# Experts' layer: four sets of tile buffers instead of two, two output buffers, weighted mask sums in other instructions, another order table

## The reference, cut to what matters

```python
q = jnp.einsum('btd,ed->bte', hidden_states, W_q)
sim = jnp.einsum('pbthn,hkpn->pbthk', q, keys)
scores_xy, idx_xy = jax.lax.top_k(sim, K)                  # K = 8 of 64 keys, twice, 4 heads
all_scores = (sx[..., :, None] + sy[..., None, :]).reshape(b, t, h, K * K)
scores, pk = jax.lax.top_k(all_scores, K)                  # 8 of the 64 pairs
de = down_embed[indices]; ue = up_embed[indices]
w = jax.nn.silu(jnp.einsum('btd,bthkd->bthk', hidden_states, de) * jax.nn.softmax(scores, axis=-1))
experts_states = jnp.einsum('bthk,bthkd->btd', w, ue)
dense = W_down @ silu(W_up @ x)                            # 512 hidden features
return dense + experts_states
```

## Time and profile before

| | |
|---|---|
| median of 3 runs | 4920.42 us (4919.32 to 4925.4) |
| the profiled execution | 4937.9 us, its span 4936.6 us |
| busy in the span | PE 86%, DVE 79%, POOL 76%, ACT 66% |
| experts' layer, first n0 to last xr | 448.4 to 1080.7 us |
| one turn of its loop in the steady state | 37.57 us |
| busy in such a turn | DVE 31.18, POOL 32.24, ACT 29.90, PE 20.61 us |
| granted clock of PE in such a turn | 0.82 |

### The profile page before, as it was taken

How to read it: one execution, slowest core, us unless ns; L and a number is a source line. 1 busy time by engine, 2 the same in 40 slices (tenths; PEclk the granted TensorE clock), 3 DMA queues, 4 the chain that set the end, 5 groups by cost and what they waited for, 6 DMA issues and landing times.

```text
span 4936.6 us, 139044 instructions
## 1 busy us (share of the span) xinstructions
PE 4239.2 (86%) x57664; PEld 3049.1 (62%) x57664; DVE 3889.2 (79%) x6375; ACT 3236.5 (66%) x5035; POOL 3775.2 (76%) x2624
## 2 busy tenths in 40 slices
PE   7886555658867899999999999999999999999997
PEld 5664444446644666666666666666666666666665
DVE  4665888855547788888888888888888888888894
ACT  4664778754434577666766767767776676767775
POOL 1113888853448899889988998889898998988993
PEclk9997778779988899999999999999999999999999
DMA  2000000000001222222222222222222222222222
GB/s 60 2 2 1 1 1 1 1 25 2 2 1 28 51 51 50 64 54 57 50 59 58 56 50 51 58 59 55 51 60 57 54 54 48 63 55 55 52 59 51
DMA packets 120832, 198.72 MB, mean 40 GB/s; under 512 B 66896, under 2 KB 78224, under 8 KB 120080
## 3 DMA queue, kind: packets, MB, share of 16 engines
q1 hardware_dynamic: 120208, 189.82, 15.7%
HBM read 24.12 MB, written 2.10 MB: 5 GB/s over the span
## 4 chain that ended last, share of the span: by engine, by line
PE 56%; ACT 14%; DVE 10%; issue 7%; POOL 6%; DMA 5%; SPq 1%; ACTq 0%; DVEq 0%; POOLq 0%
PE ps L1305 8%; PE ps L1249 8%; PE ps L1250 7%; DMA arena<-arena 5%; PE ps L1258 5%; DVE arena L1488 3%; PE ps L1346 3%; PE ps L1357 3%; PE ps L1296 2%; PE ps L1340 2%; PE ps L1297 2%; ACT L1392 2%; PE ps L1277 2%; DVE arena L1481 2%; DVE arena L598 2%
## 5 line engine op out<-in xcount | busy, mean ns | idle before, releaser
L1581 POOL TENSOR_TENSOR arena<-arena 128x1024 f32<-128x1024 f32 x384 | 909.1, 2368 | 247.7 <-DVE arena L1481 247.3
L1576 POOL TENSOR_TENSOR arena<-arena 128x32 f32<-128x32 f32 x192 | 1045.5, 5445 | 0.1
L1480 DVE TENSOR_TENSOR arena<-ps,arena 128x1024 f32<-128x1024 f32 x384 | 470.3, 1225 | 325.5 <-ACT arena L1375 325.4
L1375 ACT ACTIVATE arena<-ps 128x1024 f32<-128x1024 f32 x384 | 393.0, 1024 | 377.6 <-PE ps L1250 373.3
L1599 POOL TENSOR_TENSOR arena<-arena 128x1536 f32<-128x1536 f32 x192 | 529.1, 2756 | 114.9 <-DVE arena L1514 114.9
L208 POOL TENSOR_SCALAR arena<-arena 128x2 f32<-128x2 f32 x256 | 86.8, 339 | 630.4 <-DVE arena L202 620.4
L1305 PE MATMUL ps<-arena 96*64 96x64 f32 x12288 | 429.5, 229 | 76.1 <-DMA arena<-arena 71.6
L1305 PEld LDWEIGHTS ps<-arena 96*64 96x64 f32 x12288 | 402.8, 142 | 107.9 <-issue 99.7
L1481 DVE TENSOR_TENSOR arena<-ps,arena 128x1024 f32<-128x1024 f32 x384 | 466.5, 1215 | 0.0
L1488 DVE TENSOR_REDUCE arena<-arena 128x32 f32<-128x2048 f32 x192 | 437.0, 2276 | 0.0
L1249 PE MATMUL ps<-arena 128*128 128x512 f32 x768 | 434.3, 648 | 0.9 <-ACT arena L1424 0.9
(11 more groups left out here) (252 smaller groups left out, 9947.3 us busy)
## 6 DMA issues: line engine op xcount, KB each, us to landing
arena<-arena SPq DMA_DIRECT2D x192, 384.0 KB, 4.4
arena<-arena SPq DMA_DIRECT2D x192, 256.0 KB, 3.7
arena<-arena SPq DMA_DIRECT2D x192, 128.0 KB, 2.3
arena<-in_dWqkv SPq DMA_DIRECT2D x18, 512.0 KB, 3.6
arena<-arena SPq DMA_DIRECT2D x96, 64.0 KB
arena<-arena SPq DMA_DIRECT2D x96, 63.5 KB
arena<-in_dWo SPq DMA_DIRECT2D x6, 512.0 KB, 5.2
arena<-in_x SPq DMA_DIRECT2D x4, 512.0 KB, 7.4
```

The source lines that it names most:

```text
L1480: dve.tensor_tensor(o1, p.rearrange("p (h e) -> p h e", h=16), bc(cs, 1, 16), ALU.mult)
L1576: pool.tensor_tensor(ss[:, 0:32], ss[:, 32:64], mhalf32, ALU.pow).then_inc(*S.rs.up())
L1581: pool.tensor_tensor(a1[:, half], a1[:, half], T2[:, half], ALU.add).then_inc(*radd[g].up())
```

## The change

Five things are changed.

1. `tiles` has four sets instead of two: A and B of even batches, A and B of odd ones (`tiles[2 * (b % 2) + t]`). All waits for the reader of an earlier batch go back one batch further.
2. The normalised output lies in two buffers `out` in place of three `U.y`; n1 waits for the xr of two batches before.
3. Each of the three sums of tr is two instructions on DVE, a multiplication by a number in place and a plain addition, with a wait between them: six instructions and five waits in place of three and two.
4. PLACE has other numbers for all pieces, so another order on each engine.
5. `load_c` begins 120 words higher.

```diff
-    batches = [Batch(stats(C), sb([128, 2]), sb([128, 2, 128]), sb([128, 256]), sb([128, 4, 256]), sb([128, 2, 128]))
+    batches = [Batch(stats(C), sb([128, 2]), sb([128, 2, 128]), sb([128, 256]), sb([128, 4, 256]))
                for _ in range(NU)]
+    out = [sb([128, 2, 128]) for _ in range(2)]
...
-                  sb([128, 4, 128])) for _ in range(2)]
+                  sb([128, 4, 128])) for _ in range(4)]
...
-    PLACE = {"n0": 0, "st0": 45, "r0": 54, "hT": 120, "spcA": 193, "piA": 301, "C1A": 370, "mxA": 384, "ixA": 430,
+    PLACE = {"st0": 0, "n0": 38, "hT": 189, "spcA": 304, "spcB": 377, "r0": 416, "piA": 417, "mxA": 511, "h": 521,
...
         def tile(piece, b, t):
-            T = tiles[t]
+            T = tiles[2 * (b % 2) + t]
             ex = views(T)[3]
             if piece in ("spcA", "spcB"):
-                if b >= 1:
-                    act.wait_ge(*gp[t].at(b))
-                    act.wait_ge(*pb[t].at(b))
+                if b >= 2:
+                    act.wait_ge(*gp[t].at(b - 1))
+                    act.wait_ge(*pb[t].at(b - 1))
...
-                dve.scalar_tensor_tensor(e[:, 0:1024], e[:, 0:1024], 16.0, e[:, 1024:2048], ALU.mult,
-                                         ALU.add).then_inc(*S.step_dve.up())
-                dve.wait_ge(*S.step_dve.now())
-                dve.scalar_tensor_tensor(e[:, 0:512], e[:, 0:512], 4.0, e[:, 512:1024], ALU.mult,
-                                         ALU.add).then_inc(*S.step_dve.up())
-                dve.wait_ge(*S.step_dve.now())
-                dve.scalar_tensor_tensor(T.R, e[:, 0:256], 2.0, e[:, 256:512], ALU.mult, ALU.add).then_inc(*tr[t].up())
+                for n, w in ((1024, 16.0), (512, 4.0), (256, 2.0)):
+                    dve.tensor_scalar(e[:, 0:n], e[:, 0:n], w, None, ALU.mult).then_inc(*S.step_dve.up())
+                    dve.wait_ge(*S.step_dve.now())
+                    dve.tensor_tensor(T.R if n == 256 else e[:, 0:n], e[:, 0:n], e[:, n:2 * n], ALU.add
+                                      ).then_inc(*(tr[t] if n == 256 else S.step_dve).up())
+                    if n > 256:
+                        dve.wait_ge(*S.step_dve.now())
...
-    C.top = C.TOTAL - LAST - 1024
+    C.top = C.TOTAL - LAST - 904
```

More of the change, by code:

```diff
@@ new lines, in phase_b @@
+    PLACE = {"st0": 0, "n0": 38, "hT": 189, "spcA": 304, "spcB": 377, "r0": 416, "piA": 417, "mxA": 511, "h": 521,
+             "ixA": 523, "c8A": 576, "mxB": 582, "spA": 595, "mrA": 597, "C1A": 599, "ixB": 632, "C1B": 646,
+             "MA": 705, "nnA": 716, "c8B": 741, "ohA": 796, "mrB": 827, "eqA": 842, "piB": 863, "upc": 865,
+             "trA": 894, "spB": 898, "pcA": 909, "onA": 913, "paA": 922, "paB": 933, "xpA": 940, "txA": 953,
+             "thA": 1012, "xpB": 1014, "eqB": 1178, "pcB": 1227, "mkA": 1229, "up": 1234, "zzB": 1240, "geA": 1249,
+             "nnB": 1295, "trB": 1298, "zzA": 1331, "txB": 1393, "ohB": 1400, "MB": 1407, "sg0A": 1411, "sMA": 1425,
+             "onB": 1438, "pbA": 1461, "gpA": 1472, "sg1A": 1520, "thB": 1521, "mkB": 1596, "pbB": 1603, "geB": 1603,
+             "sg2A": 1646, "sg3A": 1647, "sg0B": 1679, "gpB": 1724, "sg1B": 2016, "atcA": 2103, "sg2B": 2213,
+             "sMB": 2295, "lsA": 2337, "sg3B": 2341, "atcB": 2470, "atA": 2494, "lsB": 2559, "st1": 2823, "n1": 2867,
+             "atB": 3155, "r1": 3250, "xr": 3453, "ot": 3459}
@@ L911, in batch @@
             if piece == "n1":
-                if b >= NU:
-                    act.wait_ge(*S.xr.at(b - NU + 1))
+                if b >= 2:
+                    act.wait_ge(*S.xr.at(b - 1))
                 act.wait_ge(*S.r1.at(b + 1))
                 p, rs = ps("ot", b), U.st[2]
-                act.activation(U.y[:, 0, :], p[:, 0:128], ACT.Identity, bias=U.nb[:, 0:1], scale=rs[:, 0:1])
-                act.activation(U.y[:, 1, :], p[:, 128:256], ACT.Identity, bias=U.nb[:, 1:2], scale=rs[:, 1:2]
+                act.activation(out[b % 2][:, 0, :], p[:, 0:128], ACT.Identity, bias=U.nb[:, 0:1], scale=rs[:, 0:1])
+                act.activation(out[b % 2][:, 1, :], p[:, 128:256], ACT.Identity, bias=U.nb[:, 1:2], scale=rs[:, 1:2]
                                ).then_inc(*S.n1.up())
         def tile(piece, b, t):
-            T = tiles[t]
+            T = tiles[2 * (b % 2) + t]
             ex = views(T)[3]
             if piece in ("spcA", "spcB"):
-                if b >= 1:
-                    act.wait_ge(*gp[t].at(b))
-                    act.wait_ge(*pb[t].at(b))
+                if b >= 2:
+                    act.wait_ge(*gp[t].at(b - 1))
+                    act.wait_ge(*pb[t].at(b - 1))
                 act.wait_ge(*sp_ps[t].at(b + 1))
@@ L989, in tile @@
         def tile(piece, b, t):
-            T = tiles[t]
+            T = tiles[2 * (b % 2) + t]
             SIM, PRJ, ey, ex, e8, eC = views(T)
             if piece in ("mxA", "mxB"):
-                if b >= 1:
-                    dve.wait_ge(*pa[t].at(b))
-                    dve.wait_ge(*C1[t].at(b))
-                    dve.wait_ge(*ix[t].at(b))
+                if b >= 2:
+                    dve.wait_ge(*pa[t].at(b - 1))
+                    dve.wait_ge(*C1[t].at(b - 1))
+                    dve.wait_ge(*ix[t].at(b - 1))
                 dve.wait_ge(*spc[t].at(b + 1))
@@ L1094, in batch @@
                 pool.wait_ge(*S.n1.at(b + 1))
-                pool.tensor_tensor(X, X, U.y, ALU.add).then_inc(*S.xr.up())
+                pool.tensor_tensor(X, X, out[b % 2], ALU.add).then_inc(*S.xr.up())
         def tile(piece, b, t):
-            T = tiles[t]
+            T = tiles[2 * (b % 2) + t]
             SIM, _, ey, ex, e8, eC = views(T)
```

78 lines of the change are left out of this document (39 added, 39 removed).

## The result

| | before | after |
|---|---|---|
| median | 4919.87 us (4918.42 to 4925.4) | 4885.85 us (4875.73 to 4890.98) |
| ratio, 95% interval | | 0.9926 [0.9908, 0.9944] |
| the same comparison again (second set of runs, on another chip) | 4931.61 us | 4887.76 us, 0.9913 [0.9900, 0.9927] |
| profiled execution, its span | 4937.9, 4936.6 us | 4875.7, 4874.4 us |
| experts' layer, first n0 to last start of xr | 448.4 to 1080.0 us | 447.4 to 1033.3 us |

The change made the kernel 34 us faster in the first comparison and 44 us in the second. The forecast was 24.6 us and a turn of 36.2. Single runs of the kernel after lie up to 15 us apart, so the layer's own time, next, measures the change better than the whole time does.

What follows compares the result with a forecast made beforehand. A loop of waits, no full engine, bounds the kernel. 14 turns from 37.57 to 36.2 (19.2 us), 1.4 at n0's third start and 4 in the drain give 24.6 us off: 4896 us, 8 in 10 within 4868 to 4927.

Steps and rivals of the forecast that it cites:

- The price of the sums: DVE's tr: six instructions taken at 2.4 us, from a range of 1.9 to 3.7, against 2.31 undisturbed for the fused three.
- a change of 0 to 0.1 us a tile: DVE's tr: what splitting the sums would change per tile, against the undisturbed 2.31 us.
- the walk: One turn of the new order followed piece by piece from the end of txA: 27.0 + r1 + 3.6, taken as 36.2 us.
- as 5.6 behind 27.0: POOL's r1 in the new turn: ends 5.6 us after st1's end at 27.0, as in the kernel before.
- spA runs 3.6: PE's spA in the new turn: takes 3.6 us behind h and hT, its copy starting 0.3 later, at 9.9.
- runs 5.45: PE's ot in the new turn: takes 5.45 us, starting 0.25 behind atcB, and ends at 26.0.
- The warning sign named for it: POOL ahead of r1: the forecast would be wrong above all if onA starts after st1.
- the rival with the queue in the products: POOL ahead of r1: late nnA puts onA, paA, paB, pcB into gpB, eqA, trA; turn 38.9, 4935 us, chance 0.14.
- R0 leaves the loop: POOL's r0: no longer closes the loop, as about 2.4 us of slack cover it before n0.
- DVE's turn: Steady turn: with r1 in 3.9 us or less DVE sets it, 34.5 us; 4870 us in all, chance 0.18.
- The drain: End of the experts' layer: DVE has 18.2 us of work in place of 22.9; 4 us counted as gain.
- If PE's clock falls under the 0.82: PE in the steady turn: a sign that the forecast is wrong, since ot and spA lie in the loop.

Runs made afterwards that it cites:

- e1: The kernel before with only four sets of tile buffers, two output buffers and load_c 120 words higher, old order and fused sums: ratio 0.9996, turn 37.38 us.
- e2: The kernel before with only the sums of tr split into six instructions: ratio 0.9954, turn 35.83 us.
- e3: The kernel after with the three fused sums put back: ratio 0.9944 to the kernel before, turn 34.80 us.
- f8: The kernel after, unchanged, run again on another chip: ratio 0.9913 to the kernel before, turn 34.09 us.
- E4: The kernel before with extra unread matmuls keeping PE busy, eight ahead of h and three behind atB: ratio 0.9957, turn 36.04 us.
- f6: The kernel after with four sets of small buffers for moments instead of three: ratio 0.9915 to the kernel before, turn 34.21 us.
- f5: The kernel after with r1 placed ahead of paA, paB and pcB on POOL: ratio 0.9927 to the kernel before, turn 34.90 us.
- g2: The kernel after with r0 alone moved ahead of oh and M on POOL: ratio 0.9942 to the kernel before, turn 36.05 us.

## Why the prediction was right, and where it was not

**Sign and range** were right: faster, within 4868 to 4927. The size was too small: 24.6 us of gain against 34 and 44 measured, and against 45.7 in the layer itself, where no other code disturbs the comparison. That 4886 lies within 10 us of the forecast 4896 is in part luck. The sum also counts 14 steady turns where its own reading of n0's starts has thirteen; with thirteen it gives 23.2 us.

**The buffers** "by themselves bring about 1 us": e1 agrees, as far as a time of 0.9996 [0.9986, 1.0006] can tell.

**The price of the sums** was right, their worth was not. The six instructions undisturbed take 0.42, 0.29 and 0.23 us for the multiplications and 0.69, 0.42 and 0.29 for the additions: 2.34 us against the 2.4 forecast. The prediction's estimate from the Trainium skill ("VectorE: DVE Perf Modes", "The perf-mode tier table") was 0.95 us for the three multiplications, and 0.94 were measured. The step that failed is "a change of 0 to 0.1 us a tile": it counted DVE's time alone. That more seams help POOL stood behind it as a remark without a number, and it was the term: e2 puts it at 1.8 us a turn in the old order, e3 at 0.7 in the new one. The rule of the same page's "Rules for kernel authors" to keep the number of chained operations low would have cost this gain (the same row also says not to fuse for performance): on DVE the split costs nothing, and beside it POOL gains.

**The order.** The step that failed is the walk's way to r1: ot, then st1 at 27.0, and r1 "as 5.6 behind 27.0". In the steady turns of after neither ot nor st1 holds r1. St1 ends at 24.7 of the walk, POOL's queue is through at 29.0, and r1, which starts 0.1 later, ends at 30.8 in place of 32.6; n1 to txA take 3.4 in place of 3.6. These are the 2.0 us between 36.2 and 34.2. The split sums are 0.7 us of it by e3 (the terms may overlap).

Two terms of the walk were taken from rows at the low clock, as if the clock belonged to the instruction: "spA runs 3.6" and ot "runs 5.45". Both came out shorter in the turn shown, spcA starts at 7.9 and not at 9.9, and ot ends at 23.0 and not at 26.0. For spA this counts: at the low level in every turn the turn would be 34.4 to 34.9 by f8's and after's own turns, so 0.3 to 0.8 of the 2.0 us. For ot it isn't shown to count, as st1 was waiting for DVE and r1 for POOL. How the rest of the 2.0 us divides stays open. E4 shows the clock by itself in the old order, where ot and spA are links of the chain: 1.6 us a turn.

**R1** was 5.6 behind the end of st1; it is 6.15, but not by a root that is held up: r1's four take 1.8 us, and the queue ahead of them 4.9. The warning sign named for it came: onA starts at 766.90, 0.2 us after st1, and not because nnA is late (it ends at 764.0) but because pcA ahead of it is held up under gpB, 2.67 us. Still the rival with the queue in the products didn't come: the queue meets eqA and two multiplications, takes 4.9 us where it has 3.3 undisturbed, and r1 still ends early, as the queue begins at 24.1 of the walk and r1's own four aren't held up.

**R0 leaves the loop**: right. Its wait fell from 30.6 to 6.3 us.

**A wait that the walk hadn't**: st0 behind n1, 1.84 us a turn. The small buffers of a batch exist three times, and st0 of batch b writes where n1 of b-3 reads. By f6 it costs nothing: it stands beside mkA's wait for txA, which takes its place when it goes.

**DVE's turn**, the first rival (34.5 us, chance 0.18), is the nearer one by the turn, 34.2. Its condition wasn't met as put (r1 in 3.9 us or less). DVE reaches the next mkA in 34.2 us all the same, with 3.0 us idle in the turn. By time the first comparison lies between the two (4896, 4886, 4870).

**The drain** gave 2.4 us where I counted 4. "The start is the same" was wrong: the first distance is 27.2 us and not 23.5. With r1 and r0 moved ahead (g1) it is 23.9 again, but the second grows by 1.5 us.

**POOL's busy time** "should stay near 32 us a turn": 28.3. The size of this fall says nothing by itself: f6 has 488 us of busy POOL in the layer where after has 454, and both have the same turn.

**The clock as a sign.** "If PE's clock falls under the 0.82" came true (0.80 in the turn of after), without what it was to warn of: ot was at the high level, and the transposes, which have slack, at the low one.

## What to carry to other kernels

Where DVE and POOL share a stretch, cost an edit on DVE by the longest instruction that POOL can meet in it, and not by DVE's sum: three fused operations split into six cost DVE nothing and took 2 us a turn off POOL. An idle microsecond of one of the two engines is the other one's slot, so filling it holds up what was there (r0 in f5, oh in g2); ask first what falls under the products then, and what stands behind that in the loop. Time between two events isn't yet a chain: st1 ended ahead of r1, and r1 didn't wait for it. A matmul's duration from a profile belongs to the clock of that place, and a new order can change it by a factor of nearly two, either way.

## What the runs showed of the hardware

**Multiplications on DVE shut POOL out too**, although they read only one tile. DVE and POOL in the turn of after:

```profile
769.45 0.86 DVE L1054 TENSOR_SCALAR arena<-arena 128x1024 bf16<-128x1024 bf16 x1
```

```profile
769.41 0.61 POOL L1110 TENSOR_TENSOR arena<-arena 128x256 f32<-128x256 f32 x1
```

POOL started 0.04 us ahead; the multiplication took 0.86 us instead of 0.42 and ended 0.29 us behind POOL's end. In 12 of 16 turns these two show the same 0.86 us within 0.01. The other way round, paB's L1111 (32 elements), which starts 0.54 us into this multiplication, takes 0.42 us in place of 0.24 and ends 0.1 us behind it, in the same 12 turns. This is what the Trainium skill says of DVE's modes with two ports ("SBUF — State Buffer", "SBUF: two separate sides"), which the prediction left open for multiplications: the trace agrees. The plain additions hold POOL up as well: pcB's L1115 starts 0.03 us into the first one (0.69 us) and takes 1.14 us in place of 0.61. So the lock isn't avoided by the split, it is only held for 0.7 us at most at a time within tr, instead of 1.2.

**The clock and the two durations.** 32 transposes take 3.84 us at the high level and up to 6.8 us in stretches with a part at the low one; spA's four matmuls of 512 columns take 2.0 and up to 3.8 us, ot 3.7 and 5.45. How long PE idled just ahead doesn't tell the level: in the kernel before, the first transposes of a turn stand behind 3.3 us of idle PE each time, and take 3.84 us in eight turns and 5.5 to 6.6 in five. In the layer the granted clock is 0.78 before and after the change alike, while ot changed its level in all steady turns and spA in half of them: the mean of a stretch doesn't say which instructions have it.
